# A selective scan's input products divided anew between VectorE and GpSimd, with matmuls of zeros between TensorE's copies

## The reference, cut to what matters

```python
def step(h, inp):
    u_, de_, b_, c_ = inp
    dA = jnp.exp(de_[..., None] * A)
    h = h * dA + (de_ * u_)[..., None] * b_[:, None, :]
    y = jnp.einsum('bdn,bn->bd', h, c_)
    return (h, y)
...
y = selective_scan(x, delta, A, Bm, Cm)
y = y + Dp[None, :, None] * x
return y * silu(z)
...
y = y_f + y_b + y_s
```

## Time and profile before

| | us |
|---|---|
| median of 3 runs | 746.49 |
| lowest, highest | 744.54, 747.54 |
| the profiled execution, its own time | 750.81 |
| span in the profile, first to last instruction | 749.0 |

### The profile page before, as it was taken

One profiled execution on the slowest core, in us unless ns is written; L12 is line 12 of the kernel. 1 busy time (PEld: TensorE's weight loads), 2 busy tenths in 40 slices (PEclk: granted clock), 3 DMA queues, 4 the chain that ended last, 5 costly groups with the idle time before them and its releaser, 6 DMA issues.

```text
span 749.0 us, 11674 instructions
## 1 busy us (share of the span) xinstructions
PE 609.9 (81%) x3947; PEld 349.8 (47%) x3947; DVE 647.5 (86%) x896; ACT 509.2 (68%) x608; POOL 427.3 (57%) x292
## 2 busy tenths in 40 slices
PE   7899998999988952577776777776757888799997
PEld 5655546677764310244443544454435653233332
DVE  7798996889976979999999899999998874788876
ACT  2658531879976767697886796888868611477673
POOL 3699993000001075798898798798986911533331
PEclk9999999999999985699998797999987999999999
DMA  2004200331001031000000000000000013100000
GB/s 58 4 13 97 37 1 8 71 95 24 4 3 60 14 84 39 1 1 0 1 1 0 1 0 1 0 1 1 0 1 0 1 46 56 42 1 0 15 1 14
DMA packets 28853, 14.98 MB, mean 20 GB/s; under 512 B 23022, under 2 KB 24942, under 8 KB 28654
## 3 DMA queue, kind: packets, MB, share of 16 engines
q1 hardware_dynamic: 27582, 13.61, 8.2%
q10 hardware_dynamic: 1216, 0.66, 0.4%
HBM read 5.14 MB, written 0.78 MB: 8 GB/s over the span
## 4 chain that ended last, share of the span: by engine, by line
PE 38%; DVE 36%; ACT 11%; issue 9%; POOL 4%; DMA 0%; DVEq 0%; SPq 0%; ACTq 0%; POOLq 0%
PE ps L588 35%; DVE arena L1397 15%; DVE ps L1069 8%; ACT arena L1639 3%; DVE arena L1069 3%; DVE arena L1115 2%; POOL arena L1800 2%; ACT arena L1753 2%; DVE ps L1115 1%; DVE arena L1284 1%; PE ps L649 1%; PE ps L770 1%; DVE arena L1348 1%; ACT arena L1740 1%; ACT ps L1740 1%
## 5 line engine op out<-in xcount | busy, mean ns | idle before, releaser
L588 PE MATMUL ps<-arena 128*32 128x64 f32 (+5 forms) x2072 | 338.4, 352 | 110.9 <-ACT arena L1753 33.6
L588 PEld LDWEIGHTS ps<-arena 128*32 128x32 f32 (+4 forms) x2072 | 123.4, 123 | 243.4 <-issue 96.2
L1800 POOL TENSOR_TENSOR arena<-arena 128x1024 f32<-128x1024 f32 x91 | 181.7, 2011 | 33.1 <-DVE arena L1397 14.4
L1397 DVE TENSOR_TENSOR_SCAN arena<-arena,ps 128x1024 f32<-128x1024 f32 x60 | 137.2, 2287 | 8.2 <-DVE ps L1069 0.5
L1785 ACT ACTIVATE arena<-ps,nycol 128x1024 f32<-128x1024 f32 x64 | 71.2, 1115 | 56.9 <-PE ps L588 56.9
L1069 DVE TENSOR_TENSOR ps<-arena,ps 128x1024 f32<-128x1024 f32 x69 | 83.8, 1214 | 9.0 <-PE ps L588 8.3
L1397 DVE TENSOR_TENSOR_SCAN arena<-ps,arena 128x1024 f32<-128x1024 f32 x36 | 81.6, 2267 | 0.1
L1740 ACT ACTIVATE arena<-arena,a_col 128x1024 f32<-128x1024 f32 x60 | 68.7, 1144 | 10.1 <-DVE arena L1397 9.7
L1924 POOL TENSOR_TENSOR arena<-arena,bmask 128x128 f32<-128x128 f32 x64 | 30.9, 485 | 77.9 <-PE ps L588 66.8
L1069 DVE TENSOR_TENSOR arena<-ps,arena 128x512 f32<-128x512 f32 (+2 forms) x75 | 48.6, 654 | 24.5 <-PE ps L588 19.7
L1639 ACT ACTIVATE arena<-arena 128x256 f32<-128x256 f32 x128 | 59.0, 504 | 6.1 <-DVE arena L1284 4.7
(11 more groups left out here) (209 smaller groups left out, 1021.0 us busy)
## 6 DMA issues: line engine op xcount, KB each, us to landing
arena<-arena SPq DMA_DIRECT2D x54, 64.0 KB
arena<-arena SPq DMA_DIRECT2D x12, 128.0 KB, 3.3
w_conv<-in_c_far SPq DMA_DIRECT2D x1, 1152.0 KB, 5.7
w_conv<-rpb_pad SPq DMA_DIRECT2D x36, 28.0 KB, 1.8
arena<-x SPq DMA_DIRECT2D x12, 64.0 KB, 2.0
arena<-x1t SPq DMA_DIRECT2D x12, 64.0 KB, 2.0
arena<-x3t SPq DMA_DIRECT2D x12, 64.0 KB, 2.0
arena<-arena SPq DMA_DIRECT2D x2, 288.8 KB, 3.7
```

The lines of the kernel that those rows point to most:

```text
L588: return pe.matmul(o, l, r, start=start, stop=stop, **k)
L1397: ve.tensor_tensor_scan(hs_ring[n % RING], decay, add, 0.0, ALU.mult, ALU.add).then_inc(S("scan"), 1)
L1800: return gp.tensor_tensor(o, a, b, ALU.mult)
```

## The change

`SHARED` becomes (3, 5, 7, 9, 11, 13, 15): seven states of sixteen, all odd. `NSH` follows it, and with it the counts of the semaphores. In `spread`, ahead of the wait that precedes a shared B, TensorE issues four matmuls of a zero matrix (`no_weight`, 96 x 128, bf16) with 512 columns of `sel`, which accumulate into bank 6; this is left out in the spreads ahead of the loop and in the one issued at n = 0. ScalarE's `copy_y` at state 3 moves from ahead of the copy of C to behind it. GpSimd clears `no_weight` at the start, as the first of its memsets, and TensorE waits for them once.

```diff
-SHARED = (3, 6, 8, 11, 13, 15)
+SHARED = (3, 5, 7, 9, 11, 13, 15)
...
+        no_weight = sb("no_weight", [P, P], BF16)
...
-            def spread(k, n):
+            pe.wait_ge(s_zero, 1)
+
+            def add_nothing(count):
+
+                for _ in range(count):
+                    mm(ps[:, 6, :], no_weight[0:96], sel[:, 0:4].rearrange("p n m -> p (n m)"),
+                       start=False, stop=False, skip_group_check=True)
+
+            def spread(k, n, accumulating=False):
...
                 if n + 2 in SHARED:
+                    if accumulating:
+                        add_nothing(4)
                     pe.wait_ge(S("c_copied"), above(k * NS + (n + 1)))
...
-                        spread(*divmod(k * NS + n + AHEAD, NS))
+                        spread(*divmod(k * NS + n + AHEAD, NS), accumulating=n > 0)
...
-                    if n == 3 and k in (1, DIRS, DIRS + 1):
-                        ac.wait_ge(S("y_acc"), above(item(k - 1, NS - 1) + 1))
-                        copy_y(0 if k == DIRS else ORDER[k - 1], slice(0, T))
...
                     ac.activation(c_ring[n % RING], bank2(4), ACT.Copy).then_inc(S("c_copied"), 1)
+                    if n == 3 and k in (1, DIRS, DIRS + 1):
+                        ac.wait_ge(S("y_acc"), above(item(k - 1, NS - 1) + 1))
+                        copy_y(0 if k == DIRS else ORDER[k - 1], slice(0, T))
...
-            for w in (w_def, w_attn[:], w_in[:], w_out[:], w_dt[:], w_low[:]):
+            for w in (no_weight[:], w_def, w_attn[:], w_in[:], w_out[:], w_dt[:], w_low[:]):
                 last = gp.memset(w, 0.0)
             last.then_inc(s_zero, 1)
```

## The result

The changed kernel takes 752.05 us in the median of 5 runs (750.9 to 753.52) against 746.45 before: 1.0074 times, 95% interval 1.0052 to 1.0096. It is 5.6 us slower, where 8.2 less were forecast.

The account below looks back on a forecast made before the run. VectorE was taken to bound the scan stage, losing time to TensorE's clock. Terms -8.2 + 3.5 + 2.4 - 5.7 gave about -8.0, with overlap -8.2: 738.3 us from the median 746.5, range 731 to 747.

Parts of the forecast that it names:

- The floor: VectorE's scan stage: one input product fewer per tile, -8.2 us, giving 47.1 us per tile and 282.7 for six.
- two thirds, -5.7: Zero matmuls on TensorE: shorter gaps keep the clock up, winning two thirds of at most 8.3 us of stalls.
- the two new stalls: VectorE waiting for GpSimd, +3.5 us, and for the later copy_y, +2.4 us; overlapping, they leave the sum at -8.2.
- Part 2: copy_y behind the copy of C: VectorE waits 1.2 us in tiles 1 and 4, +2.4 us, range 0 to 7.6.
- The chain: Tiles 1 and 4: copy of C, matmuls, transposes, copy_y, turning back, B for state 4; 6.9 us against 5.7 available.
- part 3: Zero matmuls where TensorE waits for a copy of C: free at the high clock, gain 0 to 8.3 us, taken -5.7.
- ScalarE's lack of room: Alternating stretch, states 3 to 15: two states take ScalarE 5.71 us against VectorE's 5.72; no separate term in the sum.
- Part 1's GpSimd term: One more GpSimd product per tile; with du at state 7, 1.2 us late in tiles 0 to 2, +3.5 us.
- The forecast that new stalls would take the place of the clock's: Scan stage: new GpSimd and ScalarE stalls replace most of the clock's; 735.5 to 742 us, chance 0.45.
- Rival D: Third part of spread: zeros run at the low clock and cost 16 us, so slower, 754 us; chance 0.1.

Follow-up runs that it names:

- the last experiment: Changed kernel with TensorE collecting before the spread for state 5, copy_y ahead again, D * u at state 15, GpSimd's du at state 14: 739.45 us, 0.9900 of before.
- The second profile of before: The kernel before, run once more with a profile and no edit: 745.09 us, stage of 298.54 us.
- the collection first: Changed kernel, but TensorE collects a tile's last state before spreading B for the next tile's state 5, copy_y ahead of the copy of C again: 744.2 us, 0.9953 of before.

## Why the prediction was wrong

**The floor was right.** "1.36 us, on the path, six times: -8.2 us" is what VectorE's work lost; two tiles of the last experiment stand on 47.15 us.

**The base was an unlucky execution.** The sum took 5.7 us out of the 8.3 of stalls of one profile and then subtracted the result from the median. The second profile of before shows that most of the 4.3 us by which the first lay above the median were these very stalls: 4.0 in place of 8.3. The step "I take two thirds, -5.7" counted time that a run near the median does not spend. (The overlap of the two new stalls that the sum names would make it -9.2 rather than -8.2; against what follows this is small.)

**Part 2 was mis-sized.** The chain was named with its links, but priced at the high level, 1.2 us in tiles 1 and 4 and nothing in tile 3, "as both tiles with the sliced direction have the high clock now". At that level the price was of the right order: 0.65 us at state 4 in both tiles of the run without zeros. In the changed kernel TensorE stands idle for 1.88 and 1.87 us within the chain, the clock falls, and the links behind are slow: 3.14 and 1.58 us in tile 1, 2.21 and 0.90 in tile 4, and 1.23 at state 6 of tile 3. That is 9.1 us, where 2.4 were taken and 7.6 was the upper bound. Undoing its order is worth 7.9 us. The three waits at state 6 do not all belong to the chain: with the collection first, 0.9 to 1.0 us of each remains, and no run says why. The low level in this chain was seen only with the zeros ahead of its gap, so part 3 of the change seems to have raised the price of part 2; that the zeros make the clock fall there is not shown.

**ScalarE's lack of room was seen and given no price.** The text says that "what ScalarE once loses there, it does not win back" and then adds nothing for what it loses in the middle of the stretch. D * u is 1.04 us at state 8 in every tile. It comes out at state 10, 0.6 to 1.9 us in five of the six tiles, 4.3 together. Moving it takes 5.3 us off the changed kernel. It stood in the description of the code (L1759), not in the sum.

**Part 1's GpSimd term came out near its size, for another reason.** 3.5 us were taken, for `du` in tiles 0 to 2. The delays by GpSimd are 2.6 us, but spread over all tiles in steps of at most 0.45, and moving `du` leaves most of them. The stall by `du` itself appeared once the larger stalls were gone: 1.9 us of waits, gone when `du` was moved. Stalls of several engines in one stretch did not add here, and what lies behind a long one could not be read from the profile in which it was hidden.

**Part 3 depends on the rest.** 5.7 us were taken for it. The zeros are worth nothing with six shared states (747.0), about 2 us in the changed kernel (754.14 without, intervals overlap), and 9.4 with the collection first. By the two profiles of the changed kernel, with and without them, they take 8 us of waits away at state 10 and add 6 at states 4 and 6.

**The rivals.** The forecast that new stalls would take the place of the clock's is what happened, at a larger size: 19.7 us over the floor instead of about 12. Rival D, slower, came near the time (754) by a cause that did not occur: it had the zeros run at the low clock, and of their 40 groups one took 1.91 us, one 1.25 and the others 1.02 or 1.03. The slower outcome came by another way, the chain and D * u together.

## What to carry to other kernels

Before a piece of work joins an engine's fixed order, list what stands behind it in that order and who waits for that; price the list at both levels of the clock, if the list makes TensorE wait. A stretch in which an engine needs as long as the bound engine, as ScalarE here with 5.71 us against 5.72, has no slack for anything that happens once: move such single pieces (an extra copy, a product for later) to where the bound engine is slow, here next to the unshared states. And take stalls for the base of a sum from more than one execution.

## What was not expected of the hardware

TensorE's clock fell after gaps of 1.88 and 1.51 us, although a group of matmuls had run just ahead of each; after another gap of 1.52 us in the same kernel as the 1.51 it did not fall, and in the kernel before one gap of 1.92 us was followed by the low level and another was not the earlier trace rows. What decides between them is open. With matmuls of a matrix of zeros the granted clock was higher in five of the stage's six tiles (0.84 instead of 0.78 in the first, 0.96 instead of 0.84 in the last), with the collection first; in the changed kernel it was higher in three.
